# Three engines' orders in a six-layer attention kernel: p before the squares, o before p·v, the sum of p behind the layer norm, and a seventh buffer for v

## The reference

```python
for i in range(DEPTH):                       # 6 layers
    x = attn_layer(x, Wqkv[i], ...) + x
    x = ffn_layer(x, ...) + x

def attn_layer(x, Wqkv, qs, ksc, Wo):        # 16 heads of 64, windows of 32
    q, k, v = split(x @ Wqkv)
    q, k = l2norm(q) * qs, l2norm(k) * ksc   # then both are turned by sin/cos tables
    sim = q @ [previous window, own window of k].T * 8, masked
    return softmax(sim) @ [same windows of v] @ Wo

def ffn_layer(x, g, bln, W1, b1, W2, b2):
    xn = layernorm(x) * g + bln
    a, gate = split(xn @ W1 + b1)            # 341 columns each
    return a * gelu(gate) @ W2 + b2
```

## Time and profile before

| | |
|---|---|
| median of 3 runs | 1866.52 us (1862.97 to 1867.11) |
| the profiled execution | 1871.32 us, of which the span of the trace is 1869.3 us |
| busy: TensorE / VectorE / GpSimd / ScalarE | 93% / 88% / 80% / 70% of the span |
| TensorE's granted clock | 0.98 of full, 1.00 or 0.99 in each 200 us from 200 to 1800 us |

### The profile page before, as it was taken

One profiled execution on the slowest core, in us unless ns is written; L12 is line 12 of the kernel. 1 busy time (PEld: TensorE's weight loads), 2 busy tenths in 40 slices (PEclk: granted clock), 3 DMA queues, 4 the chain that ended last, 5 costly groups with the idle time before them and its releaser, 6 DMA issues.

```text
span 1869.3 us, 48666 instructions
## 1 busy us (share of the span) xinstructions
PE 1741.2 (93%) x18122; PEld 1137.8 (61%) x18122; DVE 1638.4 (88%) x2782; ACT 1316.0 (70%) x2362; POOL 1503.7 (80%) x1204
## 2 busy tenths in 40 slices
PE   8779999999999999999999999999999999999986
PEld 7356666566665666666666666666666666566563
DVE  5799999998989989988899899889899998998873
ACT  3566777767777777677677777776777777777762
POOL 4788888888888888878888888888888888888860
PEclk8799999999999999999999999999999999999998
DMA  4022222222322222222223222222222222222220
GB/s 111 21 70 71 68 62 66 59 70 67 81 58 67 65 56 77 72 63 68 61 58 82 63 71 70 59 58 73 71 72 63 66 60 57 55 69 57 55 63 28
DMA packets 155273, 120.59 MB, mean 65 GB/s; under 512 B 42607, under 2 KB 151457, under 8 KB 154913
## 3 DMA queue, kind: packets, MB, share of 16 engines
q1 hardware_dynamic: 155041, 117.48, 24.4%
HBM read 18.79 MB, written 1.05 MB: 11 GB/s over the span
## 4 chain that ended last, share of the span: by engine, by line
PE 51%; DVE 27%; SPq 7%; ACT 6%; issue 5%; DMA 3%; POOL 0%; DVEq 0%; ACTq 0%
PE qk_bank L376 11%; PE ring_bank L448 7%; PE ring_bank L389 5%; PE ring_bank L472 5%; PE ring_bank L516 5%; PE sc_bank L423 4%; SPq L1180 4%; PE ring_bank L399 3%; DVE ss L824 3%; DVE rn L842 3%; DVE step L837 3%; PE ring_bank L461 3%; ACT sq L618 3%; DVE o L898 3%; PE ring_bank L527 3%
## 5 line engine op out<-in xcount | busy, mean ns | idle before, releaser
L1052 POOL TENSOR_TENSOR turned<-qkn,tables 128x512 f32<-128x512 f32 x384 | 490.0, 1276 | 245.3 <-DVE qkn L850 231.6
L1059 POOL TENSOR_TENSOR turned<-qkn,tables 128x512 f32<-128x512 f32 x384 | 499.4, 1300 | 0.0
L376 PE MATMUL qk_bank<-wqkv,xT 128*128 128x512 f32 x768 | 368.4, 603 | 13.3 <-DVE qkn L858 13.1
L1088 POOL TENSOR_TENSOR turned<-turned 128x512 f32<-128x512 f32 x192 | 253.3, 1319 | 15.1
L690 ACT ACTIVATE oT<-ring_bank 128x512 f32<-128x512 f32 x192 | 114.7, 597 | 210.9 <-PE ring_bank L461 210.0
L1095 POOL TENSOR_TENSOR turned<-turned 128x512 f32<-128x512 f32 x192 | 244.3, 1273 | 15.0
L448 PEld LDWEIGHTS ring_bank<-vw,pT 128*32 128x32 f32 x6144 | 157.2, 110 | 146.9 <-issue 146.7
L824 DVE TENSOR_REDUCE ss<-sq 128x16 f32<-128x1024 f32 x192 | 232.0, 1208 | 7.6 <-ACT sq L618 7.6
L654 ACT ACTIVATE kB<-ring_bank 64x512 f32<-64x512 f32 x384 | 227.2, 592 | 5.3 <-PE ring_bank L410 2.6
L898 DVE TENSOR_TENSOR o<-ring_bank,rr 128x512 f32<-128x512 f32 x192 | 132.9, 692 | 95.7 <-PE ring_bank L448 93.7
L448 PE MATMUL ring_bank<-vw,pT 128*32 128x128 f32 x6144 | 208.4, 276 | 1.7 <-issue 0.7
(11 more groups left out here) (169 smaller groups left out, 3217.2 us busy)
## 6 DMA issues: line engine op xcount, KB each, us to landing
vw<-vs SPq DMA_DIRECT2D x1152, 64.0 KB, 2.1
vw<-vs SPq DMA_DIRECT2D x672, 32.0 KB, 1.9
wqkv<-in_L_ffn_Wqkv_dram SPq DMA_DIRECT2D x20, 384.0 KB, 3.4
wo<-in_L_ffn_Wo_dram SPq DMA_DIRECT2D x20, 128.0 KB, 3.3
w<-in_L_ffn_W_dram SPq DMA_DIRECT2D x6, 341.0 KB, 3.2
wqkv<-in_L_ffn_Wqkv_dram SPq DMA_DIRECT2D x1, 1536.0 KB, 10.3
x<-in_x_dram SPq DMA_DIRECT2D x2, 512.0 KB, 4.6
out_dram<-x SPq DMA_DIRECT2D x4, 256.0 KB, 2.3
```

The costliest lines, as they stand in the source:

```text
L376: mm = pe.matmul(QK[u % 2][:, i * UW:(i + 1) * UW], tok, wqkv[:, layer % 2, cut:cut + UW], start=True, stop=True)
L1052: return pool.tensor_tensor(heads(turned[:, u % 2, 2 * i, :]), heads(qkn[:, u % 2, i * UW:(i + 1) * UW]), table.unsqueeze(1).to_broadcast( ...
L1059: return pool.tensor_tensor(halves(turned[:, u % 2, 2 * i + 1, :]), halves(qkn[:, u % 2, i * UW:(i + 1) * UW])[:, :, ::-1, :], table.rearr ...
L1088: pool.tensor_tensor(q, q, turned[:, u % 2, 1, :], ALU.add).then_inc(q_summed, 1)
```

## The change

Four edits.

1. `vs` has seven places instead of six, and the copy of v waits for the DMAs of unit u-5 instead of u-4.
2. TensorE transposes o of unit n-6 directly behind the v projection, ahead of p·v and the scores. Since the banks are dealt out in this order, the turns are now v, o, p·v, p, k, X, q.
3. ScalarE squares q and k behind the copies of p and k, instead of ahead of them.
4. In slot 3 VectorE sums p behind the layer norm. In the other seven slots it stays ahead of `scale_o`.

```diff
-VS = 6
+VS = 7
...
                 values(n)
+                transpose_o(n - 6)
                 attend(n - 5)
                 scores(n - 3)
-                transpose_o(n - 6)
                 transpose_p(n - 4)
...
-                    act.wait_ge(vw_dma[u % 2], vw_count(u - VS + 2))
+                    act.wait_ge(vw_dma[(u - VS + 2) % 2], vw_count(u - VS + 2))
...
                 copy_oT(n - 6)
-                squares(n)
                 copy_pT(n - 4)
                 if s == 3:
                     gelu(g - 2, 0)
                     gelu(g - 2, 2)
                 copy_kB(n - 2)
+                squares(n)
...
-                sum_p(n - 4)
+                if s != 3:
+                    sum_p(n - 4)
                 scale_o(n - 5)
                 if s == 3:
                     layer_norm(g - 2)
+                    sum_p(n - 4)
```

## The result

| | before | changed |
|---|---|---|
| median | 1866.82 us (4 runs, 1862.97 to 1868.62) | 1887.37 us (4 runs, 1881.27 to 1889.37) |
| ratio to before, with its 95% interval | | 1.0097 (1.0070 to 1.0124) |
| the profiled execution, its span | 1871.32, 1869.3 us | 1881.27, 1879.3 us |

The changed kernel is 1% slower. The forecast was 1882 us with a range of 1862 to 1893.

The account below looks back on a forecast made before the run. GpSimd and VectorE pace each other, 0.97 us idle per unit as floor. 22 groups x 0.84 = 18.5 us, less 2 for DMAs and 0.5 for the end, gives 16.0 more: median 1882 us, range 1862 to 1893.

Parts of the forecast that it names:

- The pace: GpSimd and VectorE hold each other up through the Newton steps, with 0.97 us of GpSimd idle per unit as floor.
- the gains would be lost: TensorE's shorter waits in slots 4, 5 and 0, 0.6 us each, costed at nothing, becoming waits for scaled q.
- the rival of closing gaps: GpSimd's gaps of 1.47 and 1.39 us in slots 4, 7, 0 fall to 0.97: 1837 us; 0.13 with TensorE-only bound.
- P7: Start of GpSimd's q and k turn behind slot 7's p·v; idle gap before it 1.39 us.
- P6: Start of GpSimd's q and k turn behind the p·v of slot 6.
- Slot 3's squares: Moved squares stand between ScalarE's Gelus and its copy of q, making that copy 0.91 us later.
- The layer norm held by GpSimd: In slot 3 it waits for GpSimd's last operation: of 0.70 us gained, 0.29 arrive.
- P2: Start of GpSimd's q and k turn behind slot 2's p·v; from there VectorE's chain runs to the next `xnT`.
- The sum: Slot 4's p·v 1.06 us later, 0.22 given back in slot 5: 0.84 us per group, 16.0 us in all.
- P4: Start of GpSimd's q and k turn behind slot 4's p·v, set by that p·v; forecast 1.06 us later.
- P5: Start of GpSimd's q and k turn behind slot 5's p·v; its gap shrinks from 1.19 to 0.97 us.
- 2 for the DMA waits: Gain from v's seventh place, as ScalarE's v copies no longer wait for DMAs: 0 to 3.4 us, taken as 2.

Follow-up runs that it names:

- only_squares: The kernel before with only the squares moved behind the copies of p and k: 1870.93 us, ratio 1.0024.

## Why the prediction held, point by point

**The pace, and that the gains would be lost.** Right. In the changed kernel's slot 5 the transposed q and the projection behind it read:

```profile
1567.20 0.63 PE L399 MATMUL ring_bank<-ident,turned 128*128 128x128 f32 x4 [0.18 <-POOL turned L1090]
1568.54 1.98 PE L376 MATMUL qk_bank<-wqkv,xT 128*128 128x512 f32 x4 [0.71 <-DVE qkn L858]
```

The wait for the copy of p has become one of 0.71 us for the scaled q, as forecast. Only "gone" was too strong: 46.0 us in 67 weight loads remain. The gaps of 1.39 stayed, so the rival of closing gaps fell. In the changed kernel without Newton steps P7's gap is 0.60 us, in the kernel before without them 1.81, so the pace was not the only thing that kept it open. That rival's price was also too small: it took 0.97 us for each of the 181 waits, though P6 has 0.29 in five layers. By the gaps it is 22 x (0.50 + 0.21 + 2 x 0.42) = 34 us, not 27.

**Slot 3's squares.** Right. From the projection up to the end of q's copy it is 8.37 us instead of 7.45: 0.92 more, forecast 0.91. P·v waits for that copy.

**The layer norm held by GpSimd.** Right. It lasts 1.04 us (forecast 1.1), and from P2 to the projection up it is 1621.38 - 1612.23 = 9.15 instead of 9.44: 0.29 less, as worked out. The rows agree with the Trainium skill ("SBUF — State Buffer", Who interferes with whom), by which a VectorE instruction with two SBUF inputs contends with a GpSimd instruction that reads SBUF while a reduction never does: in the kernel before, the sum of p took 0.67 us beside GpSimd's operation; in the changed kernel the layer norm, which now overlaps the end of that operation, took 1.04.

**The sum.** Per group, from P2 to P4, 11.04 + 9.94 = 20.98 us instead of 19.88: 1.10 more (forecast 1.06). P5 gave back 0.16 to 0.21 (forecast 0.22). Together 0.93 instead of 0.84. Over the run, between the points that have rows:

| from, to | before | changed | difference |
|---|---|---|---|
| first layer projection to first layer norm | 162.66 | 163.68 | +1.0 |
| 20 groups, layer norm to layer norm | 1462.46 | 1478.17 | +15.7 |
| from there to the end of the span | 186.72 | 185.23 | -1.5 |

The 15.7 us are 20 x 0.93 = 18.6 less 2.9. Before, the 20 groups had 1462.46 - 20 x 72.95 = 3.5 us of disturbances, now 1478.17 - 20 x 73.88 = 0.6. I had taken 2 for the DMA waits; the edit alone measured 1.1 with zero inside its interval, so it isn't shown that all 2.9 are its work. The total from the first projection on is +15.2 us, forecast +16.0. The span of 1878 to 1889 us given around the forecast doesn't come out of its own terms: they add up to 1880 to 1891. The measurement lies in both.

**What the prediction had not seen.** First, the sum of squares, late by 1.17 us, holds the gated product `uT` behind it in slot 3, and in the new turns of the banks the transposed o of slot 4 writes the bank that this product reads: TensorE waited 0.58 us for it (1629.09). I had followed the bank of p·v and not the one of o, and wrote that the wait for the exponentials would cover this. It cost nothing, because p·v waited for q's copy until 1629.75 anyway. With edit 3 alone, where p·v has that bank, it cost a part of 0.2 us. Second, the median moved by 20.5 us, where the forecast had 15.5. The agreement of 15.2 with 16.0 is partly luck of the two profiled executions: 1871.32 us is more than the kernel before usually takes, even for its granted clock (eleven executions at 0.983 had a median of 1869.95). At equal mean clock the loss is 19 to 21 us: 1881.27 against 1862.1 at 0.989, 1888.0 against 1867.8 at 0.984, 1888.2 against 1866.8 at 0.985 (one or two executions of the changed kernel against three to six of the other). That is about 22 x 0.93 = 20.5 us with next to nothing given back. So the mechanism was right, the group was sized 0.09 us too low, and the 2.5 us taken off for the DMAs and the end are not shown.

## What the runs showed of the hardware that was not expected

**Different starts.** The first layer's q,k projection starts at 57.46 us in the profiled execution of before and at 52.22 in that of the changed kernel, though the code ahead of it is the same. One row of TensorE in the small cross attention, of before:

```profile
30.57 3.62 PE L334 MATMUL qk_bank<-vw,uT 77*128 77x128 f32 x16
```

and of the changed kernel:

```profile
30.55 1.95 PE L334 MATMUL qk_bank<-vw,uT 77*128 77x128 f32 x16
```

The same 16 matmuls take 3.62 or 1.95 us. The granted clock of the stretch, `PEclk` behind the busy times, first of before, then of the changed kernel:

```profile
30.50:42.50 12.00, 12.00 (x63) 12.00 (x62) 3.06 (x5) 2.98 (x5) 0.00 (x0) 0.54 0.14 12
```

```profile
30.50:42.50 12.00, 9.56 (x86) 9.34 (x84) 8.16 (x27) 2.66 (x5) 2.53 (x4) 1.00 0.14 12
```

0.54 of 2.4 GHz is the 1.2 GHz level for nearly all of the 12 us, and 1.00 is the 2.4 GHz level. Just ahead TensorE ran the same transposes in both, with waits of 0.28 to 1.13 us in before and of 0.45 to 0.80 in the changed kernel. The code behind it comes 43.79 - 38.55 = 5.2 us later (line 345, the last of its three groups, in the two traces). One and the same program seems to have both starts, though only one execution of each is traced: the mean granted clock was 0.989 in the changed kernel's profiled execution, of 1881.27 us, and 0.984 or 0.985 in its three others, of 1886.55 to 1889.37. For before it was the other way round: its profiled execution had 0.983 and is 4.8 us above the median. So a difference of 5 us between two single executions of this kernel says nothing of an edit, and counting from the first projection takes the start out, but no other difference between two executions. There are starts between the two: only_squares was granted 0.64 in this stretch, and its first projection starts at 56.45 us. What decides which start an execution gets, no run shows.

**Standing still is not a matter of size.** An instruction of 16 columns stood still as long as one of 512 did: the Newton step took 1.11 us beside GpSimd and 0.17 without, 0.94 more, and `rstd` 1.65 instead of 0.69, 0.96 more. And it works both ways. Beside VectorE's `dsq` and `rstd` GpSimd's operations took 1.72 and 1.59 us instead of 1.27 (1617.29 and 1619.09 above).

**What a held instruction needs after its release.** The layer norm ended 0.54 and 0.56 us behind GpSimd's end, whether it had started 1.10 or 0.48 us before that. Freely it takes 0.74.

## What to carry to other kernels

Where the longest wait is a regular one between two engines, the waits of the others are slack, and shortening them turns them into new waits: first find what makes the regular one (here small VectorE instructions with two SBUF inputs, blocked beside GpSimd's, and free once written as reductions), and only then try the rest again, since the value of the other edits can change in sign or size with it, as that of the seventh place did here. When the order in which shared banks are dealt out changes, write down for each user which read it now waits for, and look up when that read ends in the slot with the most work; one slot of eight made the whole loss here. A move that costs in one slot can be left out there.
